# Seven of the eight late output-projection tiles as three fp32r products, in a fused attention and mixture-of-experts kernel on one Trainium2 core; the first expert tile's parts made beside them

## The chip, the core and the metric

The kernel runs on one core of a Trainium2 chip. A core has five engines that run side by side and meet by semaphores: TensorE (PE) multiplies matrices into PSUM banks, VectorE (DVE), ScalarE (ACT) and GpSimd (POOL) work on rows of 128 partitions, and SyncE (SP) issues transfers. SP, ACT and POOL each issue transfers on a queue of their own. The metric is the device time of one launch in microseconds (us).

## The reference

The layer computes, for x of shape (2, 1024, 512):

```python
xn = _layernorm(x, axis=-1)
x = x + _L0_attn_ref(xn, w_attn, b_attn, w_proj, b_proj) + _L0_ffn_ref(xn, gate_w, w1, w2)
```

The attention has 16 heads of 32 with rotary factors, a causal mask and a softmax that is scaled by 512 ** -0.5 after it; its heads are joined and projected: `o @ w_proj + b_proj`. The feed-forward part sends each of the 2048 tokens to the best 2 of 8 experts; an expert computes `silu(x w1_gate) * (x w1_up)` with 352 hidden columns and then `@ w2`, and the two results are added with the router's weights. Inputs and output are fp32.

## The kernel before, in words

The program has three blocks, one behind the other, with a barrier of all engines between them: `project_qkv` (layernorm, q, k, v, routing choice), `attend` (scores, softmax, values, and the output projection of the first sequence's eight tiles of 128 tokens), and `experts`. The change is in `experts`.

`experts` begins with the output projection of the second sequence: `LATE` = 8 tiles of 128 tokens. For each, PE multiplies `o_t` (attention output, transposed, four groups of 128 rows) by `w_proj` in four fp32 products of 512 columns (L990; the trace shows two records for each), DVE adds the residual to the bank and writes the sum back into `o_t` (L912), and ACT issues the transfer of the sum to the accumulator in HBM (L865). The banks are the four `gu` banks of the expert tiles, in turn.

Behind it come 39 expert tiles of 128 routed rows. An fp32 product is done there as three fp32r products: each operand is split into a high part (ACT casts it to fp32r, `copy`) and a low part (DVE subtracts the high part from the value), and high x high, high x low and low x high are added in PSUM. For expert tile i, PE turns the rows (`turn_rows`, L927), ACT makes `rows_hi` (L818), DVE `rows_lo` (L883); the expert's w1 is split in four pieces `w1_hi` (ACT, L822) and `w1_lo` (DVE, L890). `up(i, r, 0)` and `up(i, r, 1)` are the gate and up products, 12 of 352 columns each (L935 to L937). Then silu (ACT, L846), the product with the up half (DVE, L906), its transposition (L945, L876, L877), the down product (L953), scaling (L834) and a scatter that adds into HBM (POOL, L801). Two sets of each buffer alternate, r = i % 2.

The order on each engine is the order in which the code is written; nothing plans it. The tail of the projection is interleaved by hand with the parts of expert tile 0: at projection tile 7 ACT makes `w1_hi` and `rows_hi` of tile 0 (L860, L861), DVE makes `w1_lo` behind the add of tile 6 (L915) and `rows_lo` behind that of tile 7 (L916). PE announces a tile's expert (`announce_tile`, L976) once SP has seen its weights land; ACT waits for `tile_ready` before it reads the slot number (L738, a load of a register from memory). SP issues the weights of experts 1 and 2 after the third and the sixth residual add (L767).

Of the kernel before, what the change touches and what calls it, by code (L numbers as in the profile page):

```python
# [18 lines left out]
ALU = mybir.AluOpType  # L19
# [653 lines left out]
def experts(nc, keep, scratch, x, b_proj, w1_t, w2_t, out):  # L673
# [6 lines left out]
    with ctx:  # L680
# [12 lines left out]
        w1_lo = [m.sbuf(f"w1_lo{r}", [P, DK, 2 * I], F32R) for r in range(2)]  # L693
        gated = m.sbuf("gated", [P, I], F32)
# [20 lines left out]
        tile_ready = m.sem("tile_ready")  # L715
        gu_full, silu_done, hidden_done = m.sem("gu_full"), m.sem("silu_done"), m.sem("hidden_done")
# [92 lines left out]
        def _(act):  # L809
# [4 lines left out]
            def rows_to_sbuf(i, r):  # L814
                act.wait_ge(turned, i + 1)
                if not early(i):
                    act.wait_ge(gu_full, 2 * (i - 1))
                nc.scalar.copy(rows_hi[r][:], turn_ps[:]).then_inc(rows_hi_done, 1)  # L818
# [5 lines left out]
            def await_up_weights(i):  # L824
                if past(i, 2):
                    act.wait_ge(gu_full, (i - 1) * 2)
                act.wait_ge(tile_ready, i + 1)
# [29 lines left out]
            nc.scalar.activation(warm[:], ident[:, 0:1], ACT.Silu).then_inc(warmed, 1)  # L857
            for a in range(LATE):
                if a == LATE - 1:
                    up_weights_high(0, await_up_weights(0), range(DK))  # L860
# [10 lines left out]
        def _(dve):  # L871
# [7 lines left out]
            def rows_low(i, r):  # L879
                dve.wait_ge(rows_hi_done, i + 1)  # L880
                if not early(i):
# [3 lines left out]
            def up_weights_low(i, r, slot, ks):  # L885
                if past(i, 2):
                    dve.wait_ge(gu_full, (i - 1) * 2)
                for k in ks:
# [18 lines left out]

            for a in range(LATE):
                at = EARLY + a
                dve.wait_ge(proj_full, a + 1)  # L910

                nc.vector.tensor_tensor(o_t[:, :, at * P:(at + 1) * P], gu[a % 2][a // 2 % 2][:].rearrange("p (g t) -> p g t", t=P),  # L912
                                        res[:, at, :].rearrange("p (g t) -> p g t", t=P), ALU.add).then_inc(res_done, 1)
                if a == LATE - 2:
                    up_weights_low(0, 0, slot_at(dve, 0), range(DK))  # L915
            rows_low(0, 0)  # L916
# [4 lines left out]
        def _(pe):  # L921
# [36 lines left out]
            def tile(i, r, half):  # L958
# [7 lines left out]
                else:  # L966
                    pe.wait_ge(res_done, LATE)
# [12 lines left out]
            pe.wait_ge(ident_done, 1)  # L980
            for a in range(LATE):
# [3 lines left out]
                if a == LATE - 2:  # L985
                    announce_tile(0)
                if a == LATE - 1:
                    turn_rows(0, 0, 0)
                for g in range(NG):
                    last = nc.tensor.matmul(gu[a % 2][a // 2 % 2][:], o_t[:, g, at * P:(at + 1) * P], wp[:, g, :],  # L990
                                            start=(g == 0), stop=(g == NG - 1))
# [614 lines left out]
```

## Time and profile before

| | |
|---|---|
| runs, us | 902.1, 902.72, 905.22 (median 902.72) |
| profiled execution | 906.29 us, span 904.6 us |
| PE busy | 820.4 us, 91% of the span |
| DVE, ACT, POOL busy | 57%, 44%, 28% |
| mean granted clock of TensorE | 0.954 of full speed |

Full speed of TensorE's clock is 2.4 GHz, the lower level 1.2 GHz. Times in the rows are from the start of the span; the block `experts` opens near 562.8 and PE's first expert product is at 595.73. A timeline row gives the start, the length (of a merged group: from its first start to its last end), engine, line, operation, output and inputs, count, and in square brackets the idle time ahead of it with what ended it. PEclk is the granted clock of a stretch.

### The profile page before, as it was taken

To read this page: it belongs to the slowest core of one execution; us is meant where nothing else is said; L and a number is where in the kernel's file an instruction comes from. 1 tells how busy PE (TensorE), PEld (TensorE's weight loads), DVE (VectorE), ACT (ScalarE), POOL (GpSimd) and SP (SyncE) were. 2 spreads that over 40 slices of the span, in tenths; PEclk is the share of its full clock that TensorE was granted. 3 is DMA by queue.
4 is the path that set the end of the run, shared out by engine and by line. 5 is a ranking of instruction groups with operands and counts; after the bars stand their busy time and mean duration, and the time that the engine had idled before them with its cause. 6 is when DMAs were issued, how large, how long until landed. Compare 5 with 4: busy or idle time off the path is not lost. (4 is left out here: it accounts for less than half of the span.)

```text
span 904.6 us, 13761 instructions
## 1 busy us (share of the span) xinstructions
PE 820.4 (91%) x3973; PEld 559.8 (62%) x3974; DVE 515.3 (57%) x1334; ACT 394.8 (44%) x779; POOL 249.4 (28%) x314
## 2 busy tenths in 40 slices
PE   3889999569989999999999998979999999999990
PEld 3768989435445555555555443458778777787860
DVE  5992543395466667666666401166666666666640
ACT  3231231104445556555555630046666655556630
POOL 3782000134132424323233251002223223222220
PEclk9899999856899999999999999999999999999995
DMA  9386695894445755597671014843663664633327
GB/s 323 144 254 198 201 320 182 269 236 144 145 148 144 229 140 160 134 234 188 180 180 56 15 57 113 278 151 70 165 160 75 168 173 73 172 71 70 70 35 208
DMA packets 80477, 143.21 MB, mean 158 GB/s; under 512 B 16688, under 2 KB 30512, under 8 KB 80368
## 3 DMA queue, kind: packets, MB, share of 16 engines
q10 hardware_dynamic: 29056, 58.28, 23.8%
q1 hardware_dynamic: 43200, 65.72, 23.6%
q0 software_dynamic: 8176, 18.65, 9.8%
q8 instruction: 22, 0.36, 0.2%
q14 instruction: 23, 0.19, 0.1%
HBM read 81.21 MB, written 61.15 MB: 157 GB/s over the span
## 5 line engine op out<-in xcount | busy, mean ns | idle before, releaser
L1340 ACT ACTIVATE probs<-scores_t 128x512 f32<-128x512 f32 (+3 forms) x384 | 163.8, 492 | 148.7 <-PE scores_t L1467 136.9
L890 DVE TENSOR_TENSOR w_lo<-w,w_hi 128x704 fp32r<-128x704 f32 x156 | 131.7, 885 | 91.1 <-ACT w_hi L822 83.7
L1444 PE MATMUL maxima<-k_stack,q_stack 96*128 96x512 f32 (+3 forms) x384 | 142.2, 391 | 15.0 <-DMA q_stack<-qk_hi 9.0
L1487 PE MATMUL o_acc<-probs,v_ones 128*64 128x512 f32 (+3 forms) x768 | 149.9, 513 | 0.0
L1467 PE MATMUL scores_t<-q_stack,k_stack 98*128 98x512 f32 (+3 forms) x384 | 138.5, 386 | 7.2 <-DMA q_stack<-row_lo 5.1
L1374 DVE TENSOR_REDUCE mx<-maxima 128x1 f32<-128x512 f32 x128 | 88.2, 689 | 89.5 <-PE maxima L1444 89.3
L1370 DVE CUSTOM_DVE_ANT_0 masked_scores<-maxima,mask_m 128x128 f32<-128x128 f32 (+3 forms) x256 | 121.5, 485 | 23.8 <-PE maxima L1444 20.7
L822 ACT CAST w_hi<-w 128x704 fp32r x156 | 114.1, 783 | 34.2 <-issue 33.5
L935 PE MATMUL gu<-w_hi,rows_hi 128*128 128x352 f32 x312 | 119.7, 384 | 5.3 <-DVE rows_lo L883 4.0
L1467 PEld LDWEIGHTS scores_t<-q_stack,k_stack 98*128 98x128 f32 x384 | 73.6, 194 | 70.0 <-issue 42.7
L953 PE MATMUL down<-w,hidden_t 128*128 (+1 forms) x234 | 108.0, 597 | 0.8 <-DVE hidden_t L877 0.8
L936 PE MATMUL gu<-w_lo,rows_hi 128*128 128x352 f32 x312 | 101.5, 325 | 0.0
L937 PE MATMUL gu<-w_hi,rows_lo 128*128 128x352 f32 x312 | 101.3, 325 | 0.0
L1444 PEld LDWEIGHTS maxima<-k_stack,q_stack 96*128 96x128 f32 x384 | 77.5, 204 | 35.8 <-issue 9.5
L1285 POOL TENSOR_SCALAR_AFFINE_SELECT probs<-probs 128x256 f32<-128x256 f32 x120 | 48.4, 406 | 145.1 <-ACT probs L1340 143.5
L1487 PEld LDWEIGHTS o_acc<-probs,v_ones 128*64 128x64 f32 x768 | 47.8, 139 | 64.5 <-issue 39.6
L834 ACT ACTIVATE y<-down,tags 128x512 f32<-128x512 f32 x39 | 26.9, 689 | 107.7 <-PE down L953 58.7
L800 POOL COPY row_index<-tags 128x1 f32 (+1 forms) x39 | 8.7, 223 | 234.2 <-ACT y L834 173.3
L935 PEld LDWEIGHTS gu<-w_hi,rows_hi 128*128 128x128 f32 x312 | 59.1, 189 | 15.4 <-DVE w_lo L890 7.7
L801 POOL DMA_INDIRECT acc<-y,row_index x39 | 63.3, 1624 | 16.8 <-issue 15.4
L953 PEld LDWEIGHTS down<-w,hidden_t 128*128 128x128 f32 (+1 forms) x234 | 42.1, 190 | 39.8 <-issue 38.3
L280 ACT ACTIVATE st_hi<-bank,small 128x512 fp32r<-128x512 f32 x32 | 21.9, 687 | 101.8 <-PE bank L537 101.8
(158 smaller groups left out, 1168.9 us busy)
## 6 DMA issues: line engine op xcount, KB each, us to landing
w<-in_w_t SPq DMA_DIRECT2D x8, 1408.0 KB, 6.6
routed<-blank_row ACTq DMA_DIRECT2D x20, 514.0 KB, 6.5
rows<-routed ACTq DMA_DIRECT2D x39, 256.0 KB, 3.5
qk_hi<-st_hi SPq DMA_DIRECT2D x32, 256.0 KB, 4.7
qk_lo<-st_lo SPq DMA_DIRECT2D x32, 256.0 KB, 6.0
q_stack<-qk_hi ACTq DMA_DIRECT2D x32, 256.0 KB, 4.1
k_stack<-qk_hi ACTq DMA_DIRECT2D x26, 256.0 KB, 4.7
v_all<-o_t SPq DMA_DIRECT2D x4, 1536.0 KB, 5.7
```

What stands on the lines that cost most here:

```text
L822: nc.scalar.copy(w1_hi[r][:, k, :], w1_rows(slot, k)).then_inc(w1_hi_done, 1)
L890: nc.vector.tensor_tensor(w1_lo[r][:, k, :], w1_rows(slot, k), as_f32(w1_hi[r][:, k, :]), ALU.subtract).then_inc(w1_done, 1)
L935: nc.tensor.matmul(out, hi, w1_hi[r][:, k, cols], start=(k == 0), stop=False)
L936: nc.tensor.matmul(out, hi, w1_lo[r][:, k, cols], start=False, stop=False)
L937: last = nc.tensor.matmul(out, lo, w1_hi[r][:, k, cols], start=False, stop=(k == DK - 1))
L953: last = nc.tensor.matmul(down[r][:], hidden_t[r][0:n, k, :], w2[0:n, bass.ds(e, 1), k, :].rearrange("p o n -> p (o n)"), start=(k == 0), ...
L1340: nc.scalar.activation(probs[:, k % PR, h, 0:w], scores_t[e % RING][:, 0:w], ACT.Exp).then_inc(exp_done, 1)
L1370: nc.vector.tensor_tensor_reduce(out=masked_scores[bank][:, 0:w], in0=scores, in1=mask_m[:, CH - w:CH], scale=1.0, scalar=NEG, op0=ALU.add ...
L1374: nc.vector.tensor_reduce(to, scores, AX.X, ALU.max).then_inc(m_free, 1)
L1444: nc.tensor.matmul(mb[at % RING][:, 0:w], q_st[i][0:3 * HD, h, t * P:(t + 1) * P], k_st[i][0:3 * HD, h, c * CH:c * CH + w], start=True, st ...
L1467: last = nc.tensor.matmul(out[:, 0:w], k_st[i][0:STACK, h, j * P:(j + 1) * P], q_st[i][0:STACK, h, t0:t0 + w], start=True, stop=not diag)
L1487: last = nc.tensor.matmul(o_acc[c][2 * HD * h:2 * HD * (h + 1), CH - w:CH], v_st[i][:, j, h:h + 2, :].rearrange("p o d -> p (o d)"), probs ...
```

## The change

The first late tile keeps its four fp32 products. Tiles 1 to 7 are computed in twelve fp32r products each, like the expert tiles. Their parts are made in `experts` itself: the high part of the tile's `o_t` goes to `rows_hi`, the low part to `rows_lo` (`projected_high`, `projected_low`, one tile ahead of PE in the code), and the projection weights' parts (`wp_hi`, `wp_lo`) are laid over set 1 of `w1_hi` and `w1_lo`. So expert tile 0 may write its rows' parts only after projection tile 6 and expert tile 1 its parts only after tile 7.

Parts of expert tile 0 move ahead: `w1_hi` on ACT behind the high part of tile 6, `w1_lo` on DVE in two halves behind the adds of tiles 5 and 6, `rows_lo` ahead of the add of tile 7. The announcement of tile 0 moves from projection tile 6 to tile 4, and PE waits for the identity only at tile 7. Expert tile 0's products wait for seven adds instead of eight.

```diff
+        wp_hi, wp_lo = (t[1][:].rearrange("p k n -> p (k n)")[:, 0:NG * D].rearrange("p (g n) -> p g n", n=D) for t in (w1_hi, w1_lo))
...
+        wp_hi_done, wp_done = m.sem("wp_hi_done"), m.sem("wp_done")
+        o_hi_done, o_done = m.sem("o_hi_done"), m.sem("o_parts_done")
...
             def rows_to_sbuf(i, r):
                 act.wait_ge(turned, i + 1)
-                if not early(i):
+                if early(i):
+                    act.wait_ge(proj_full, LATE - 1 + i)
+                else:
                     act.wait_ge(gu_full, 2 * (i - 1))
...
             def await_up_weights(i):
                 if past(i, 2):
                     act.wait_ge(gu_full, (i - 1) * 2)
+                elif i == 1:
+                    act.wait_ge(proj_full, LATE)
                 act.wait_ge(tile_ready, i + 1)
...
+            def projected_high(a):
+                at = EARLY + a
+                if a > 2:
+                    act.wait_ge(proj_full, a - 1)
+                nc.scalar.copy(rows_hi[a % 2][:].rearrange("p (g t) -> p g t", t=P), o_t[:, :, at * P:(at + 1) * P]).then_inc(o_hi_done, 1)
+
+            projected_high(1)
+            for g in range(NG):
+                nc.scalar.copy(wp_hi[:, g, :], wp[:, g, :]).then_inc(wp_hi_done, 1)
             for a in range(LATE):
+                if 1 <= a < LATE - 1:
+                    projected_high(a + 1)
+                if a == LATE - 3:
+                    up_weights_high(0, await_up_weights(0), range(DK))
                 if a == LATE - 1:
-                    up_weights_high(0, await_up_weights(0), range(DK))
                     rows_to_sbuf(0, 0)
                     load_rows(2, 0)
...
             def rows_low(i, r):
                 dve.wait_ge(rows_hi_done, i + 1)
-                if not early(i):
+                if early(i):
+                    dve.wait_ge(proj_full, LATE - 1 + i)
+                else:
...
             def up_weights_low(i, r, slot, ks):
                 if past(i, 2):
                     dve.wait_ge(gu_full, (i - 1) * 2)
+                elif i == 1:
+                    dve.wait_ge(proj_full, LATE)
...
+            def projected_low(a):
+                at = EARLY + a
+                dve.wait_ge(o_hi_done, a)
+                if a > 2:
+                    dve.wait_ge(proj_full, a - 1)
+                nc.vector.tensor_tensor(rows_lo[a % 2][:].rearrange("p (g t) -> p g t", t=P), o_t[:, :, at * P:(at + 1) * P],
+                                        as_f32(rows_hi[a % 2][:]).rearrange("p (g t) -> p g t", t=P), ALU.subtract).then_inc(o_done, 1)
+
+            projected_low(1)
+            for g in range(NG):
+                dve.wait_ge(wp_hi_done, g + 1)
+                nc.vector.tensor_tensor(wp_lo[:, g, :], wp[:, g, :], as_f32(wp_hi[:, g, :]), ALU.subtract).then_inc(wp_done, 1)
             for a in range(LATE):
                 at = EARLY + a
+                if 1 <= a < LATE - 1:
+                    projected_low(a + 1)
                 dve.wait_ge(proj_full, a + 1)
...
+                if a == LATE - 4:
+                    first = slot_at(dve, 0)
+                if a == LATE - 3:
+                    up_weights_low(0, 0, first, range(0, DK // 2))
                 if a == LATE - 2:
-                    up_weights_low(0, 0, slot_at(dve, 0), range(DK))
-            rows_low(0, 0)
+                    up_weights_low(0, 0, first, range(DK // 2, DK))
+                    rows_low(0, 0)
...
                 if past(i, 2):
                     pe.wait_ge(hidden_done, i - 1)
                 else:
-                    pe.wait_ge(res_done, LATE)
+                    pe.wait_ge(res_done, LATE - 1 + i)
...
-            pe.wait_ge(ident_done, 1)
             for a in range(LATE):
                 at = EARLY + a
                 if a >= 4:
                     pe.wait_ge(res_done, a - 3)
-                if a == LATE - 2:
+                if a == LATE - 4:
                     announce_tile(0)
                 if a == LATE - 1:
+                    pe.wait_ge(ident_done, 1)
                     turn_rows(0, 0, 0)
+                bank = gu[a % 2][a // 2 % 2]
+                if a:
+                    pe.wait_ge(o_done, a)
                 for g in range(NG):
-                    last = nc.tensor.matmul(gu[a % 2][a // 2 % 2][:], o_t[:, g, at * P:(at + 1) * P], wp[:, g, :],
-                                            start=(g == 0), stop=(g == NG - 1))
+                    if a == 0:
+                        last = nc.tensor.matmul(bank[:], o_t[:, g, at * P:(at + 1) * P], wp[:, g, :],
+                                                start=(g == 0), stop=(g == NG - 1))
+                        continue
+                    if a == 1:
+                        pe.wait_ge(wp_done, g + 1)
+                    hi, lo = (t[a % 2][:, g * P:(g + 1) * P] for t in (rows_hi, rows_lo))
+                    nc.tensor.matmul(bank[:], hi, wp_hi[:, g, :], start=(g == 0), stop=False)
+                    nc.tensor.matmul(bank[:], hi, wp_lo[:, g, :], start=False, stop=False)
+                    last = nc.tensor.matmul(bank[:], lo, wp_hi[:, g, :], start=False, stop=(g == NG - 1))
                 last.then_inc(proj_full, 1)
```

PE at the opening of the block, before: fp32 products (`gu<-w_proj,o_t`), the first of them behind the identity.

```order
L920 UNCONDITIONAL_BRANCH [waits barrier_Pool_Activation_PE_DVE_SP_release]
L990 MATMUL gu<-w_proj,o_t 128x512 [waits ident3_done]
L990 MATMUL gu<-w_proj,o_t 128x512 x15
L990 MATMUL gu<-w_proj,o_t 128x512 [waits res_done]
L990 MATMUL gu<-w_proj,o_t 128x512 x3
L990 MATMUL gu<-w_proj,o_t 128x512 [waits res_done]
L990 MATMUL gu<-w_proj,o_t 128x512 x3
```

PE there after the change; `o_parts_done` counts tiles whose parts of `o_t` are made, `wp_done` the pieces of the projection weights.

```order
L961 UNCONDITIONAL_BRANCH [waits barrier_Pool_Activation_PE_DVE_SP_release]
L1035 MATMUL gu<-w_proj,o_t 128x512 x4
L1041 MATMUL gu<-w_hi,rows_hi 128x512 [waits wp_done,o_parts_done]
L1042 MATMUL gu<-w_lo,rows_hi 128x512
L1043 MATMUL gu<-w_hi,rows_lo 128x512
L1041 MATMUL gu<-w_hi,rows_hi 128x512 [waits wp_done]
L1042 MATMUL gu<-w_lo,rows_hi 128x512
L1043 MATMUL gu<-w_hi,rows_lo 128x512
L1041 MATMUL gu<-w_hi,rows_hi 128x512 [waits wp_done]
```

The wait for the identity is gone from the first product, and the second tile's products wait for parts from ACT and DVE instead.

ACT, from the table load to the first expert tile's parts, before:

```order
L857 ACT_TABLE_LOAD
L857 ACTIVATE warm<-ident 128x1 [waits ident3_done]
L865 DMA acc<-o_t 512x1x128 [waits res_done] x7
L738 TENSOR_LOAD tile_slot [waits tile_ready]
L738 ISA x2
L822 ISA
L822 COPY w_hi<-w 128x704
L822 ISA
L822 COPY w_hi<-w 128x704
```

ACT there after the change, the opening:

```order
L864 ACT_TABLE_LOAD
L864 ACTIVATE warm<-ident 128x1 [waits ident3_done]
L869 CAST rows_hi<-o_t 128x512
L873 CAST w_hi<-w_proj 128x512 x4
L884 DMA acc<-o_t 512x1x128 [waits res_done]
L869 CAST rows_hi<-o_t 128x512
L884 DMA acc<-o_t 512x1x128 [waits res_done]
L869 CAST rows_hi<-o_t 128x512 [waits proj_full]
```

and from the high part of projection tile 6 to the parts of expert tile 1, after the change:

```order
L827 ISA
L827 COPY w_hi<-w 128x704
L827 ISA
L827 COPY w_hi<-w 128x704
L884 DMA acc<-o_t 512x1x128 [waits res_done]
L869 CAST rows_hi<-o_t 128x512 [waits proj_full]
L884 DMA acc<-o_t 512x1x128 [waits res_done]
L823 CAST rows_hi<-turn_ps 128x512 [waits proj_full,rows_turned]
L815 DMA rows<-routed 128x512
L884 DMA acc<-o_t 512x1x128 [waits res_done]
L741 TENSOR_LOAD tile_slot [waits tile_ready,proj_full]
L741 ISA x2
```

Each transfer of a sum now has a cast of the next tile's `o_t` behind it on ACT, and the four `w_hi<-w` casts stand ahead of the last three transfers instead of the last one.

DVE at the end of the projection, before:

```order
L738 TENSOR_LOAD tile_slot
L738 ISA x2
L890 ISA [waits w1_hi_done]
L890 TENSOR_TENSOR w_lo<-w,w_hi 128x704
L890 ISA [waits w1_hi_done]
L890 TENSOR_TENSOR w_lo<-w,w_hi 128x704
L890 ISA [waits w1_hi_done]
L890 TENSOR_TENSOR w_lo<-w,w_hi 128x704
L890 ISA [waits w1_hi_done]
L890 TENSOR_TENSOR w_lo<-w,w_hi 128x704
L912 TENSOR_TENSOR o_t<-gu,x_rows 128x4x128 [waits proj_full]
L883 TENSOR_TENSOR rows_lo<-turn_ps,rows_hi 128x512 [waits rows_hi_done]
```

DVE there after the change:

```order
L913 ISA [waits w1_hi_done]
L913 TENSOR_TENSOR w_lo<-w,w_hi 128x704
L913 ISA [waits w1_hi_done]
L913 TENSOR_TENSOR w_lo<-w,w_hi 128x704
L936 TENSOR_TENSOR rows_lo<-o_t,rows_hi 128x512 [waits proj_full,o_hi_done]
L949 TENSOR_TENSOR o_t<-gu,x_rows 128x4x128 [waits proj_full]
L913 ISA [waits w1_hi_done]
L913 TENSOR_TENSOR w_lo<-w,w_hi 128x704
L913 ISA [waits w1_hi_done]
L913 TENSOR_TENSOR w_lo<-w,w_hi 128x704
L904 TENSOR_TENSOR rows_lo<-turn_ps,rows_hi 128x512 [waits proj_full,rows_hi_done]
L949 TENSOR_TENSOR o_t<-gu,x_rows 128x4x128 [waits proj_full]
```

The `w_lo<-w` subtractions are split by a low part and an add, and the `rows_lo<-turn_ps` subtraction stands ahead of the last add instead of behind it.

## Rows read from the trace of the kernel before

**Rows 1.** Windows: busy us of each engine, clock, DMA share, GB/s.

```profile
700.00:800.00 100.00, 100.00 (x511) 78.81 (x509) 67.49 (x112) 59.49 (x98) 26.30 (x27) 1.00 0.57 138
```

**Rows 2.** Timeline, PE: start, us, operation, count, [idle before].

```profile
563.52 24.30 PE L990 MATMUL gu<-w_proj,o_t 128*128 128x512 f32 x56 [2.63 <-POOL ident L787]
587.65 0.60 PE L927 MATMUL turn_ps<-ident,rows 128*128 128x128 f32 x4
588.09 3.60 PE L990 MATMUL gu<-w_proj,o_t 128*128 128x512 f32 x8
595.73 0.43 PE L935 MATMUL gu<-w_hi,rows_hi 128*128 128x352 f32 x1 [4.04 <-DVE rows_lo L883]
...
598.98 0.94 PE L927 MATMUL turn_ps<-ident,rows 128*128 128x128 f32 x4
...
603.21 0.40 PE L935 MATMUL gu<-w_hi,rows_hi 128*128 128x352 f32 x1 [1.30 <-DVE w_lo L890]
...
605.21 0.49 PE L945 MATMUL hid_ps<-ident,hidden 128*128 128x128 f32 x3
```

**Rows 3.** Timeline, DVE, around the last output product.

```profile
567.26 0.69 DVE L912 TENSOR_TENSOR o_t<-gu,x_rows 128x512 f32<-128x512 f32 x1 [5.64 <-PE gu L990]
...
591.17 3.30 DVE L890 TENSOR_TENSOR w_lo<-w,w_hi 128x704 fp32r<-128x704 f32 x4 [2.63 <-ACT w_hi L822]
594.39 0.68 DVE L912 TENSOR_TENSOR o_t<-gu,x_rows 128x512 f32<-128x512 f32 x1
594.99 0.68 DVE L883 TENSOR_TENSOR rows_lo<-turn_ps,rows_hi 128x512 fp32r<-128x512 f32 x1
```

**Rows 4.** Timeline, ACT and its queue, same stretch.

```profile
565.17 0.20 ACT L857 ACTIVATE warm<-ident 128x1 f32<-128x1 f32 x1
...
595.11 0.53 ACTq L865 DMA_DIRECT2D acc<-o_t  x1
596.62 1.46 ACT L822 CAST w_hi<-w 128x704 fp32r x2 [3.08 <-issue]
599.22 0.46 ACT L846 ACTIVATE gated<-gu 128x352 f32<-128x352 f32 x1 [1.14 <-PE gu L937]
```

**Rows 5.** Timeline, PE, stage one: fp32r products of 512 columns.

```profile
119.79 0.40 PE L536 MATMUL bank<-xt_lo,w_hi 128*128 128x512 f32 x1
...
125.80 0.39 PE L535 MATMUL bank<-xt_hi,w_hi 128*128 128x512 f32 x1
```

**Rows 6.** Timeline, stage one: ACT's and DVE's part making.

```profile
43.42 1.65 ACT L257 CAST w_hi<-w_raw 128x512 fp32r<-128x512 f32 x3
...
45.44 1.88 DVE L357 TENSOR_TENSOR w_lo<-w_raw,w_hi 128x512 fp32r<-128x512 f32 x3
```

**Rows 7.** Groups by form, DVE, 0 to 100 us.

```profile
L351 DVE TENSOR_TENSOR w_raw<-w_proj,o_t 128x512 f32<-128x512 f32 x8 | 7.5, 974 | 0.0
```

**Rows 8.** Timeline, POOL and SP: the block's opening, weight load.

```profile
562.81 0.21 POOL L785 MEMSET ident<- 128x128 f32 x1 [15.78 <-POOLq L1051]
...
574.84 0.37 SPq L756 DMA_DIRECT2D w<-in_w_t  x1
...
575.80 0.47 SPq L758 DMA_DIRECT2D w<-in_w_t  x1
```

**Rows 9.** Timeline, PE: other idle stretches over 1.3 us.

```profile
58.27 0.50 PE L535 MATMUL bank<-xt_hi,w_hi 128*128 128x512 f32 x1 [1.72 <-DVE st_lo L464]
...
62.66 0.51 PE L535 MATMUL bank<-xt_hi,w_hi 128*128 128x512 f32 x1 [1.34 <-DVE st_lo L464]
...
232.72 0.50 PE L1467 MATMUL scores_t<-q_stack,k_stack 98*128 98x512 f32 x1 [1.98 <-DMA q_stack<-row_lo]
...
261.52 0.61 PE L1444 MATMUL maxima<-k_stack,q_stack 96*128 96x512 f32 x1 [2.36 <-DVE mx L1370]
```

**Rows 10.** Windows: columns as in rows 1.

```profile
230.00:240.00 10.00, 8.02 (x34) 4.68 (x32) 4.37 (x14) 3.58 (x9) 2.58 (x5) 0.72 0.26 97
596.00:598.00 2.00, 2.00 (x9) 2.00 (x9) 0.45 (x1) 1.38 (x2) 0.00 (x0) 0.56 0.45 135
```

## The prediction

> **What bounds the kernel now.** I read in this order: the busy table by stretches, the timeline of TensorE (PE) around the block change, then DVE and ACT in that stretch, then older stages for prices. In the expert tiles PE is busy the whole 100 us [rows 1], one tile every 7.2 us; whatever moves the start of expert tile 1 moves the end by as much, and nothing behind it has slack to give back. So the question is when tile 1 starts. In the trace it is 603.21. Before it PE shows: idle 2.63 until the POOL identity is ready (563.52), 56 + 8 passes of the fp32 output product (64 records for 8 tiles, so 8 records a tile and 24.30 / 56 x 8 = 3.43 us a tile with the turn of 0.44 left out), end of the stream near 591.5 (588.09 + 3.43), idle 4.04 behind DVE's rows_lo, tile 0, idle 1.30 behind DVE's w_lo [rows 2]. The idle 4.04 is on DVE: four w_lo subtractions (591.17, 3.30) stand ahead of the last residual add (594.39) and rows_lo (594.99) [rows 3]. Tile 1's parts then start only after the last transfer issue of ACT at 595.11 [rows 4].
>
> **Product by product.** A 128x512 fp32r product is in stage one: 26 of them from 119.79 to 125.80 are 0.231 us apart [rows 5]. Twelve make 2.77 us against 3.43, so seven tiles save 7 x 0.66 = 4.6 us of PE work. The first tile stays fp32, and starts without the identity: the block opens at about 562.85 (POOL's first record there is 562.81 [rows 8]), not 563.52, 0.65 earlier.
>
> TensorE: Matmul & The Clock Gate, "Back-to-back issue gap", in the Trainium skill gives about 131 ns for each sustained 512-column product. By that twelve would take 1.6 us and the other two engines would pace everything; rows 5 show 231 ns here, and I do not use it.
>
> **New work on ACT and DVE.** Each product tile now needs a high part (ACT cast 128x512 from SBUF, single 0.62; three in 1.65, so 0.515 apart when queued) and a low part (DVE subtraction of SBUF tiles, three in 1.88, 0.63 apart, about 0.68 alone) [rows 6]. No trace shows the strided reads of o_t by the cast; bounds: 0.57 (a PSUM cast would be no worse) is close to 0.62, and for DVE the slow case is 0.97 for an all-SBUF 128x512 operation while other engines were busy [rows 7]. I take 0.62 and 0.68, since here POOL is idle, and keep 0.97 for a rival.
>
> The opening: ACT issues two row loads, loads its table and warms up to 565.37 [rows 4]. High part of tile 1 ready at 565.9, of the four weight pieces at 566.4, 566.9, 567.5, 568.0. DVE: low of tile 1 at 566.6, weight pieces at 567.25, 567.9, 568.5, 569.1. PE ends tile 0 at 562.85 + 3.43 = 566.28 and starts tile 1 at 567.3: stall 1.0. It then finds every piece in time and ends at 570.1. But DVE's four weight subtractions delay the residual add of tile 0 to 569.05; ACT issues its transfer (0.53) only after that add, and the high part of tile 2 stands behind the issue. 569.74 + 0.03 + 0.53 + 0.03 + 0.62 + 0.02 + 0.68 + 0.06 = 571.7. PE stalls 1.6 more.
>
> Steady: from the end of product tile a to the parts of tile a+2 there is PE to DVE 0.31 (567.26 less the end of the stream 566.95), add 0.69, issue 0.03 + 0.53, cast 0.03 + 0.62, subtraction 0.02 + 0.68, to PE 0.06: 2.97. PE works on tile a+1 meanwhile for 2.77. So it stalls 0.2 at tiles 4 and 6, 0.4 in all. The loop on DVE and ACT itself is 2.6 a tile, just below PE's 2.77.
>
> Product tile 7: ACT has four w_hi casts of 128x704 (3.0 us with the slot load ahead) between the high parts of tiles 6 and 7. They end at 585.9, high 586.4, low 587.1; PE has ended tile 6 at 585.96 and turned rows until 586.4: stall 0.8. Sum: 562.85 + 3.43 + 7 x 2.77 + 0.44 + stalls 1.0 + 1.6 + 0.4 + 0.8 = 589.9. So the product stream ends only 1.6 us earlier than 591.5: of 5.3 us saved (4.6 + 0.65), 3.8 go into new stalls.
>
> **Expert tile 0.** DVE's w_lo of this tile are split (two after the add of tile 5, two after that of tile 6, ending 589.3), rows_lo ends at 589.95. PE starts tile 0 at 590.0: the idle 4.04 is gone, 5.7 us earlier than 595.73. Its announcement is asked for at product tile 4 (577.4); SP raises it after the weight load that follows the third add. That was issued at 574.84 and took 1.4 us [rows 8]; with the third add ending at 575.5 it is raised at 577.0, in time by 0.4.
>
> **Expert tile 1: what is late next.** Its w1 parts share storage with the projection weights' parts, so ACT waits for the last product. The add of tile 7 now comes when its product ends: 589.9 + 0.31 + 0.69 = 590.95, transfer issue to 591.5, and w_hi 0.98 later (595.64 to 596.62 in the trace, with a slot load between) [rows 4]: 592.5. Two casts to 593.95, silu 0.46 [rows 4], rows_hi (0.58), two casts to 596.3, then the w_lo pair ends 597.4 and PE starts at 597.5. Tile 0 itself takes 2.0 + 0.4 + 2.0 at full clock and ends at 594.4. PE idles 3.1 us where it idled 1.30. Gain at tile 1: 603.2 - 597.5 = 5.7 us.
>
> **The clock.** The granted clock in the trace falls to its lower level (1.2 of 2.4 GHz) behind idle 1.98, 2.36 and 4.04 us, and stays up behind 1.34, 1.72 and also 2.63 [rows 2, 9, 10]. Idle 4.04 made the first half of tile 0 take 3.25 us (595.73 to 598.98) against 2.00 for tile 1's (603.21 to 605.21), and the turn 0.94 against 0.60: 1.6 in all. That loss is hidden in the old start of tile 1 only partly, because DVE and ACT set it; I count none of it twice. The new idle 3.1 ahead of tile 1 is longer than five of these six, three of the four from 1.98 up were followed by a fall, and from tile 1 on PE is the only limit: I expect one fall there. Price: between 0 and 3.4 us (in the stretch 230 to 240 the mean clock is 0.72, a longer fall), I take 1.3, a little under 1.6, as a part can pass while PE still waits. So the gain is 5.7 - 1.3 = 4.4 us.
>
> The profiled execution took 906.29 (span 904.6); the same less 4.4 is 901.9. The median of the runs is 902.72, 3.6 under it; I take the same 4.4 off that: **898.3**. A difference under 0.3% (2.7 us) cannot be told from none.
>
> **Rivals.** First, the clock stays up, as behind idle 2.63: gain 5.7, time 897.0. For it, one of the four idles from 1.98 up; against it, the other three.
>
> Second, the two helper engines become the pace. If the subtraction takes 0.97 as in rows 7, the loop is 0.69 + 0.56 + 0.65 + 0.99 = 2.9 a tile, over 2.77, the opening ends some 1.2 later and tile 7 about 2.5 later in all; with an issue of 0.61 rather than 0.53 a further 0.5. The gain is 5.7 - 3.0 = 2.7, 1.4 after the fall of the clock: 900.0 to 901.3. For it: the margin is only 0.15 a tile. Against: those slow rows stand beside POOL and heavy transfers.
>
> Third, slower: the clock falls already in the opening. Two stalls of 1.0 and 1.6 lie within 5 us. If they count as one long idle, product tiles run at half clock, 5.5 us instead of 2.77. A fall as long as that of the stretch 230 to 240 costs up to 3.4, and another of that size at tile 1 gives 6.8 against 5.7: 903.8. It decides from the point at which more than 11.4 us of PE's work run at the lower clock (each costs half of itself). Against it: the stalls 1.72 and 1.34 at 58.27 and 62.66 lie 4 us apart like these and the clock stayed up [rows 9]. The Trainium skill speaks for it in TensorE: Matmul & The Clock Gate, "A second HAM failure mode: psum-queue depth-cycling": frequent small idles between groups of products make the clock swing. Rows 9 show two that did not.
>
> Fourth, the change doesn't do what it says: the three products are not faster than the fp32 one, as when each waits for its weight load (above 0.286 each). PE would then pace the projection at 3.43, most new stalls would vanish in it, the product stream ends near 591.9 and tile 0's parts are still ready early: gain about 3.7 without, 2.4 with a fall. Against it: rows 5, the same operation at 0.231.
>
> **How the numbers follow.** Forecast 0.42, clock stays up 0.28, helpers pace 0.18, slower 0.06, not faster products 0.06. The helpers' case lies half within 0.3%. Range 895.8 to 901.4: below 897.0 by a margin for cheaper stalls (0.4 + 0.8), above to the helpers' case with a fall. Faster by over 0.3% (under 900.0): 0.42 x 0.97 + 0.28 + 0.18 x 0.4 + 0.03 = 0.79; within 0.3%: 0.16; slower 0.05.
>
> **What would show it.** Product tiles of 2.77 us on PE; stalls of about 1.0 and 1.6 ahead of product tiles 1 and 2, released by DVE, and 0.8 ahead of tile 7; almost none ahead of expert tile 0; about 3 ahead of expert tile 1, released by DVE w_lo, and half clock behind it. Tile 1 should start 5.7 us earlier (597.5), and the rest of the span should be the old 301.4 us plus what the clock takes. I am wrong if the starts of product tiles lie more than 2.9 apart after the opening, if PE waits long ahead of expert tile 0, or if something after tile 1 stalls PE that does not now.

## The result, and the profile after

In the comparison that the prediction was made for, the changed kernel has a median of 901.13 us (16 runs, 894.68 to 906.31) against 906.95 for the kernel before (16 runs, 901.9 to 912.2) on the same chips: a ratio of 0.9933, 95% interval 0.9912 to 0.9954. By the ratio that is 6 us less. Two more comparisons of the same kernel, below, gave 0.9986 (0.9953 to 1.0018) and 0.9922 (0.9897 to 0.9948). The mean of the three is 0.9947, 4.8 us of 907. The profiled execution has a span of 899.4 us, against 904.6.

All times below that are to be compared between executions are counted from POOL's first record in the block (562.81 before [rows 8], 561.21 after), since the block opened anywhere between 557.60 and 566.53 us in ten profiles of kernels that are alike up to there. I call D1 the time from there to the first product of expert tile 1: 603.21 - 562.81 = 40.40 before [rows 2, 8], 595.97 - 561.21 = 34.76 after. The timeline of PE after (start, length, operation, count, idle ahead):

```profile
561.25 5.37 PE L1035 MATMUL gu<-w_proj,o_t 128*128 128x512 f32 x8 [1.97 <-PEq L1103]
566.05 0.79 PE L1041 MATMUL gu<-w_hi,rows_hi 128*128 128x512 f32 x1
...
570.11 0.50 PE L1041 MATMUL gu<-w_hi,rows_hi 128*128 128x512 f32 x1 [0.72 <-DVE rows_lo L936]
...
575.89 0.50 PE L1041 MATMUL gu<-w_hi,rows_hi 128*128 128x512 f32 x1
...
581.73 0.47 PE L1041 MATMUL gu<-w_hi,rows_hi 128*128 128x512 f32 x1
...
584.57 0.60 PE L968 MATMUL turn_ps<-ident,rows 128*128 128x128 f32 x4
585.54 0.50 PE L1041 MATMUL gu<-w_hi,rows_hi 128*128 128x512 f32 x1 [0.37 <-DVE rows_lo L936]
...
588.40 0.37 PE L976 MATMUL gu<-w_hi,rows_hi 128*128 128x352 f32 x1
...
595.97 0.40 PE L976 MATMUL gu<-w_hi,rows_hi 128*128 128x352 f32 x1 [3.08 <-DVE w_lo L913]
...
598.99 0.84 PE L986 MATMUL hid_ps<-ident,hidden 128*128 128x128 f32 x3
```

Product tiles start at 561.25, 566.05 and 570.11, then at 573.00, 575.89, 578.75 and 581.73, which is 2.86 to 2.98 us apart; the turn of the rows is at 584.57 and tile 7 at 585.54. Expert tile 0 follows at 588.40 without an idle, where 4.04 stood before [rows 2]. The idle ahead of expert tile 1 is 3.08 instead of 1.30. The timeline of DVE after, against [rows 3]:

```profile
564.32 0.69 DVE L936 TENSOR_TENSOR rows_lo<-o_t,rows_hi 128x512 fp32r<-128x512 f32 x1 [4.31 <-ACT rows_hi L869]
564.93 2.49 DVE L942 TENSOR_TENSOR w_lo<-w_proj,w_hi 128x512 fp32r<-128x512 f32 x4
567.34 0.68 DVE L949 TENSOR_TENSOR o_t<-gu,x_rows 128x512 f32<-128x512 f32 x1
569.36 0.69 DVE L936 TENSOR_TENSOR rows_lo<-o_t,rows_hi 128x512 fp32r<-128x512 f32 x1 [1.34 <-ACT rows_hi L869]
...
584.79 0.69 DVE L936 TENSOR_TENSOR rows_lo<-o_t,rows_hi 128x512 fp32r<-128x512 f32 x1 [0.75 <-ACT rows_hi L869]
...
587.61 0.68 DVE L904 TENSOR_TENSOR rows_lo<-turn_ps,rows_hi 128x512 fp32r<-128x512 f32 x1
588.60 0.69 DVE L949 TENSOR_TENSOR o_t<-gu,x_rows 128x512 f32<-128x512 f32 x1 [0.31 <-PE gu L1043]
591.93 1.69 DVE L913 TENSOR_TENSOR w_lo<-w,w_hi 128x704 fp32r<-128x704 f32 x2 [2.64 <-ACT w_hi L827]
593.54 0.68 DVE L904 TENSOR_TENSOR rows_lo<-turn_ps,rows_hi 128x512 fp32r<-128x512 f32 x1
594.14 1.68 DVE L913 TENSOR_TENSOR w_lo<-w,w_hi 128x704 fp32r<-128x704 f32 x2
```

The four subtractions of weight pieces (564.93) hold the first residual add until 567.34. Product tile 2 waits for the subtraction at 569.36, tile 7 for that at 584.79. `rows_lo` of expert tile 0 (587.61) is ahead of the last add (588.60) now. From 591.93 DVE works without an idle until the last `w_lo` of expert tile 1 ends at 595.82, just ahead of PE's start at 595.97. ACT after, against [rows 4]:

```profile
568.05 0.61 ACTq L884 DMA_DIRECT2D acc<-o_t  x1
568.71 0.62 ACT L869 CAST rows_hi<-o_t 128x512 fp32r<-128x512 f32 x1 [2.34 <-DVE o_t L949]
...
589.32 0.53 ACTq L884 DMA_DIRECT2D acc<-o_t  x1
590.58 0.78 ACT L827 CAST w_hi<-w 128x704 fp32r x1 [3.25 <-issue]
...
591.27 0.78 ACT L827 CAST w_hi<-w 128x704 fp32r x1
...
592.77 2.82 ACT L827 CAST w_hi<-w 128x704 fp32r x4
```

The cast at 568.71 stands behind the issue at 568.05, which waited for the first add; that is the chain add, issue, cast, subtraction of the prediction. The issue at 589.32 and the first w_hi cast of expert tile 1 at 590.58 are 1.26 apart; the four casts from 592.77 are 0.68 apart and 0.78 long, and the first two of them are the last for that tile, so ACT is done with it at 594.23. The windows after (busy us of PE, PEld, DVE, ACT, POOL, then granted clock, DMA share, GB/s):

```profile
592.90:596.00 3.10, 0.03 (x1) 0.06 (x1) 3.10 (x5) 2.69 (x4) 0.00 (x0) 1.00 0.35 121
596.50:600.00 3.50, 3.50 (x16) 3.42 (x15) 1.49 (x3) 0.46 (x1) 0.00 (x0) 0.53 0.00 0
600.00:603.00 3.00, 3.00 (x18) 2.60 (x17) 2.19 (x5) 1.95 (x3) 0.00 (x0) 0.98 0.29 87
```

While PE waits for tile 1 the clock is up (1.00); it falls to its lower level (1.2 GHz) only after tile 1 has begun (0.53 on average in 596.50 to 600.00), and is up again from 600 on (0.98). Against full speed these stretches lack 3.5 x 0.47 + 3.0 x 0.02 = 1.7 us of clock. From tile 1's first product to the last down product there are 873.68 - 595.97 = 277.7 us, against 276.0 before (879.20 - 603.21).

### The profile page after: what moved, and what is told of

The parts are those of the page before. It is cut to its first block and busy times, and to the rows that moved or that the text cites. A ratio compares the mean times of both kernels' runs of the same rounds, so it can differ in the third digit from the quotient of the medians.

```text
span 899.4 us, 13854 instructions
## 1 busy us (share of the span) xinstructions
PE 817.4 (91%) x4001; PEld 565.6 (63%) x4002; DVE 521.5 (58%) x1345; ACT 401.2 (45%) x790; POOL 251.0 (28%) x314
```

## The experiments

| kernel | D1 | tile 1 to last down product | ratio to before (95%) |
|---|---|---|---|
| before | 40.40 | 276.0 | |
| changed | 34.76 | 277.7 | 0.9933 (0.9912 to 0.9954) |
| e1, fp32r products alone | 39.39 | 276.0 | 0.9962 (0.9936 to 0.9989) |
| e2, moved parts alone | 35.41 | 276.3 | 0.9949 (0.9921 to 0.9976) |
| e3, changed, transfers on SP | 31.93 | 276.1 | 0.9884 (0.9857 to 0.9911) |
| e4, changed, filler products | 34.68 | 276.1 | 0.9941 (0.9916 to 0.9965) |
| e5, e2, transfers on SP | 33.90 | 276.3 | 0.9938 (0.9900 to 0.9976) |
| e6, e3 with room of its own | 29.75 | 276.2 | 0.9869 (0.9826 to 0.9912) |
| changed, again | 34.70 | 277.6 | 0.9986 (0.9953 to 1.0018) |
| changed, third | 34.71 | 277.4 | 0.9922 (0.9897 to 0.9948) |

**e1: the products alone.** On ACT and DVE the parts of expert tile 0 go back to where they were:

```diff
-                if a == LATE - 3:
+                if a == LATE - 1:
                     up_weights_high(0, await_up_weights(0), range(DK))
-                if a == LATE - 1:
                     rows_to_sbuf(0, 0)
...
-                if a == LATE - 4:
-                    first = slot_at(dve, 0)
-                if a == LATE - 3:
-                    up_weights_low(0, 0, first, range(0, DK // 2))
                 if a == LATE - 2:
-                    up_weights_low(0, 0, first, range(DK // 2, DK))
-                    rows_low(0, 0)
+                    up_weights_low(0, 0, slot_at(dve, 0), range(DK))
+            rows_low(0, 0)
```

> The changed kernel with one part undone: the parts of expert tile 0 are made where they were before (w1_hi on ACT at projection tile 7, w1_lo on DVE behind the add of tile 6, rows_lo behind the last add); the products stay fp32r. Measure: D1, the time from POOL's first record in the block to the first product of expert tile 1; 40.4 us in the kernel before, 34.8 in the changed one. Theory (the moved parts bring most, since the saved PE time goes into new stalls): the projection ends about 1 us earlier than before, the idle of about 4 us ahead of expert tile 0 is back, D1 near 38.5 to 39.5, so 1 to 2 us of 5.6; device time 0.1 to 0.2% under the kernel before, not to be told from it. Rival (the faster products bring most of it): D1 near 36, and an idle ahead of tile 0 of under 2 us.

The timeline of PE:

```profile
562.15 0.47 PE L1036 MATMUL gu<-w_hi,rows_hi 128*128 128x512 f32 x1 [0.84 <-DVE w_lo L941]
...
566.49 0.50 PE L1036 MATMUL gu<-w_hi,rows_hi 128*128 128x512 f32 x1 [1.33 <-DVE rows_lo L935]
...
588.94 0.66 PE L971 MATMUL gu<-w_hi,rows_hi 128*128 128x352 f32 x1 [4.70 <-DVE rows_lo L903]
...
596.99 0.40 PE L971 MATMUL gu<-w_hi,rows_hi 128*128 128x352 f32 x1 [1.44 <-DVE w_lo L912]
```

The new stalls of 0.84 and 1.33 are there and the idle ahead of expert tile 0 is 4.70. D1 is 39.39, 1.0 less than before, of which 0.67 is the earlier start (0.71 behind POOL's record before, 0.04 now). The ratio looks like 3.4 us (its interval goes from 1.0 to 5.8) where 1 to 2 were expected, more than the 1.0 at D1. Its profile has 341.8 us from the opening to the end of the span, like the kernel before (341.8): behind the last down product there are 26.5 us where there were 25.4, in a stretch that the change does not touch.

**e2: the moved parts alone.** The kernel before, with the parts of expert tile 0, its announcement and the wait for the identity where the change puts them; the products stay fp32.

```diff
             for a in range(LATE):
+                if a == LATE - 3:
+                    up_weights_high(0, await_up_weights(0), range(DK))
                 if a == LATE - 1:
-                    up_weights_high(0, await_up_weights(0), range(DK))
                     rows_to_sbuf(0, 0)
...
+                if a == LATE - 4:
+                    first = slot_at(dve, 0)
+                if a == LATE - 3:
+                    up_weights_low(0, 0, first, range(0, DK // 2))
                 if a == LATE - 2:
-                    up_weights_low(0, 0, slot_at(dve, 0), range(DK))
-            rows_low(0, 0)
+                    up_weights_low(0, 0, first, range(DK // 2, DK))
+                    rows_low(0, 0)
...
-                    pe.wait_ge(res_done, LATE)
+                    pe.wait_ge(res_done, LATE - 1 + i)
...
-            pe.wait_ge(ident_done, 1)
...
-                if a == LATE - 2:
+                if a == LATE - 4:
                     announce_tile(0)
                 if a == LATE - 1:
+                    pe.wait_ge(ident_done, 1)
```

> The kernel before with the other part alone: all eight projection tiles stay fp32, and the parts of expert tile 0, its announcement and the wait for the identity are moved as in the changed kernel. Theory: the eight products stay back to back, 8 x 3.43 + 0.44 from 0.05 behind the opening, the idle ahead of expert tile 0 is under 0.5 us, and tile 1 starts 7.5 us behind the last projection product: D1 35.3 to 36, so some 4.5 to 5 of the 5.6 us; ratio to the kernel before 0.993 to 0.997. Rival (the products bring it): D1 above 38.

```profile
559.37 24.27 PE L995 MATMUL gu<-w_proj,o_t 128*128 128x512 f32 x56 [1.96 <-PEq L1056]
...
594.74 0.40 PE L940 MATMUL gu<-w_hi,rows_hi 128*128 128x352 f32 x1 [2.87 <-DVE w_lo L891]
```

The fp32 products run back to back from 559.37, no idle stands ahead of expert tile 0, and D1 is 35.41: 5.0 of the 5.65 us, of which 0.67 is the earlier start again (0.71 behind POOL's record before, 0.04 here). The rival, that the products bring the gain, has fallen.

**e3: the issue out of ACT's way.** The eight transfers of the sums move to SP.

```diff
-                act.wait_ge(res_done, a + 1)
-                act.dma_start(acc_rows[at], o_t[:, :, at * P:(at + 1) * P]).then_inc(acc_started, 16)
...
+            load_weights(0)
+            for a in range(LATE):
+                at = EARLY + a
+                sp.wait_ge(res_done, a + 1)
+                sp.dma_start(acc_rows[at], o_t[:, :, at * P:(at + 1) * P]).then_inc(acc_started, 16)
+                if a == 2:
+                    load_weights(1)
+                    announce(0)
+                if a == 5:
+                    load_weights(2)
```

> The changed kernel with the eight transfers of the sums issued by SP instead of ACT, so that ACT's cast of the next tile's high part waits for neither the residual add nor the issue (0.53 us). Theory (the new stalls come from the chain add, issue, cast, subtraction, and the start of expert tile 1 from the last add and issue ahead of its casts): stalls ahead of projection tiles 2, 4 and 6 vanish (1.2, 0.3 and 0.3 us in the changed kernel), the one ahead of tile 7 shrinks below 0.5, expert tile 1 starts 6 to 6.5 us behind the last projection product instead of 7.6: D1 31 to 32.5, against 34.8. Time 0.2 to 0.4% under the changed kernel. Rival (DVE paces the projection, and tile 1 waits for DVE in any case): D1 above 34.

```profile
566.57 5.37 PE L1037 MATMUL gu<-w_proj,o_t 128*128 128x512 f32 x8 [1.97 <-PEq L1105]
...
574.52 0.39 PE L1043 MATMUL gu<-w_hi,rows_hi 128*128 128x512 f32 x1
...
580.67 0.47 PE L1043 MATMUL gu<-w_hi,rows_hi 128*128 128x512 f32 x1 [0.55 <-SPq L766]
...
592.24 0.38 PE L978 MATMUL gu<-w_hi,rows_hi 128*128 128x352 f32 x1
...
598.46 0.40 PE L978 MATMUL gu<-w_hi,rows_hi 128*128 128x352 f32 x1 [1.64 <-DVE w_lo L915]
```

The stalls ahead of product tiles 2 and 7 are gone, and expert tile 1 starts 6.2 us behind the end of the projection (592.24 to 598.46) instead of 7.6 (588.40 to 595.97). D1 is 31.93, 2.8 less than in the changed kernel. The ratio is 0.5% under that of the changed kernel where 0.2 to 0.4 was expected; the two ratios come from different comparisons. One thing I had not expected: PE idles 0.55 at product tile 4 for SP. SP announces expert 0 only behind the weights of expert 1, as before, but now has the issue of a transfer ahead of those. The prediction had put the margin of this announcement at 0.4 us in the changed kernel; it held there. The clock fell in the opening of this execution too, and here it shows: product tile 2, which waits for nobody, starts 7.99 us behind the opening, against 7.46 in e6 below, where the clock stayed up. SP's issue of the third sum, for which that announcement waits, ends 0.39 later than in e6 (12.14 and 11.75 us behind the opening). So I estimate that some 0.4 us of e3's D1 is the clock.

**e4: fill the idle.** Twelve products whose result is overwritten stand between the halves of expert tile 0.

```diff
+                if isinstance(i, int) and i == 0:
+                    for k in range(3 * DK):
+                        nc.tensor.matmul(gu[1][0][:, 0:I], rows_hi[0][:, k % DK * P:(k % DK + 1) * P],
+                                         w1_hi[0][:, k % DK, 0:I], start=(k == 0), stop=(k == 3 * DK - 1))
                 up(i, r, 1)
```

> The changed kernel with twelve filler products of 352 columns put between the two halves of expert tile 0 (their result is overwritten; nothing reads it), to fill 2.0 of the 3.1 us for which PE waits ahead of expert tile 1. Theory (the idle makes the clock fall in tile 1): D1 stays within 0.4 us of 34.8, the clock stays up behind it, and the stretch from tile 1's first product to the end of the span is 301 to 302 us instead of 303.4; time about 0.2% under the changed kernel. Rival (the fall comes from something else, or costs nothing at the end): the stretch stays at 303.4.

```profile
590.39 2.17 PE L1017 MATMUL gu<-w_hi,rows_hi 128*128 128x352 f32 x12
...
595.65 0.40 PE L976 MATMUL gu<-w_hi,rows_hi 128*128 128x352 f32 x1 [1.18 <-DVE w_lo L913]
```

and the window behind:

```profile
595.00:600.00 5.00, 4.35 (x29) 4.35 (x30) 3.95 (x7) 3.31 (x6) 0.00 (x0) 1.00 0.06 4
```

D1 stays (34.68), the idle is 1.18, the clock stays up, and the stretch from tile 1 to the last down product is 276.1 us instead of 277.7. So the fall behind the idle of 3.1 us costs 1.6 us. By the measure of the expectation, from tile 1 to the end of the span, it is 302.15 against 303.43, or 1.3 us; I count to the last down product because what lies behind it differs by up to 0.8 us between executions of the changed kernel alone (25.7, 26.5 and 25.9). The ratio, 0.9941, does not resolve this: its interval spans 4.4 us.

**e5: fp32 products, transfers on SP.** e2 with the edit of e3.

> The kernel with fp32 projection products and the moved parts (e2), and the transfers of the sums issued by SP as in e3. It tells what the fp32r products are worth once ACT no longer stands in their way. Measure: D1, the time from POOL's first record of the block to the first product of expert tile 1 (before 40.4, changed kernel 34.8, e2 35.4, e3 31.9). Theory (in the changed kernel the saved PE time was eaten by the chain over ACT's issue; freed of it the three products pay their arithmetic): projection ends at 28.0 as in e2, tile 1 starts 6.2 to 6.3 us behind it as in e3, D1 34.2, so e3 is 2.3 us better by its products. Rival (the products pay nothing in any case, SP's issue is the whole gain of e3): D1 near 32.

```profile
559.10 24.34 PE L997 MATMUL gu<-w_proj,o_t 128*128 128x512 f32 x56 [1.97 <-PEq L1058]
...
583.71 3.60 PE L997 MATMUL gu<-w_proj,o_t 128*128 128x512 f32 x8
...
592.96 0.40 PE L942 MATMUL gu<-w_hi,rows_hi 128*128 128x352 f32 x1 [1.29 <-DVE w_lo L893]
```

D1 is 33.90. Against e3's 31.93 the fp32r products are worth 2.0 us where ACT's issue is out of the way, and 35.41 - 34.76 = 0.65 where it is not. The 2.0 are rather too few: e3 also carries the estimated 0.4 us of the clock and the wait for SP.

**e6: room of its own for the weight parts.** e3 with three edits; DVE's half of the tile gets the same two changes (no wait for the last projection product, and `first`).

```diff
-        wp_hi, wp_lo = (t[1][:].rearrange("p k n -> p (k n)")[:, 0:NG * D].rearrange("p (g n) -> p g n", n=D) for t in (w1_hi, w1_lo))
+        wp_hi, wp_lo = (m.sbuf(name, [P, NG, D], F32R) for name in ("wp_hi", "wp_lo"))
...
-                    load_weights(1)
                     announce(0)
+                    load_weights(1)
...
-                elif i == 1:
-                    act.wait_ge(proj_full, LATE)
...
-                    up_weights_high(1 - r, slot, range(0, DK // 2))
+                    first = DK if isinstance(i, int) and i == 0 else DK // 2
+                    up_weights_high(1 - r, slot, range(0, first))
```

> e3 with three edits on what then waits last: the projection weights' parts get buffers of their own (16 KB a partition) in place of set 1 of w1_hi and w1_lo, so that expert tile 1's w1 parts wait for no projection product and all four are made ahead of the silu and the rows' parts of tile 0 and 1; and SP announces expert 0 ahead of issuing the weights of expert 1 (in e3 PE idles 0.55 us for that announcement at projection tile 4). Theory (what is left ahead of tile 1 is the w1 parts' wait for the last projection product, and then 0.5 us of DVE work): no idle at projection tile 4, idle ahead of expert tile 1 0.3 to 0.8 us instead of 1.64, D1 29.7 to 30.5 against 31.9 of e3. Time 0.1 to 0.3% under e3, 1.2 to 1.5% under the kernel before. Rival (the silu of tile 0 and the rows' parts set the start of tile 1, not the w1 parts): D1 above 31.

```profile
564.21 0.47 PE L1041 MATMUL gu<-wp_hi,rows_hi 128*128 128x512 f32 x1 [0.84 <-DVE wp_lo L942]
...
567.12 0.50 PE L1041 MATMUL gu<-wp_hi,rows_hi 128*128 128x512 f32 x1
...
584.14 0.38 PE L976 MATMUL gu<-w_hi,rows_hi 128*128 128x352 f32 x1
...
589.41 0.43 PE L976 MATMUL gu<-w_hi,rows_hi 128*128 128x352 f32 x1 [0.76 <-DVE rows_lo L905]
```

DVE at the same place:

```profile
584.34 0.69 DVE L949 TENSOR_TENSOR o_t<-gu,x_rows 128x512 f32<-128x512 f32 x1 [0.30 <-PE gu L1043]
585.45 3.30 DVE L912 TENSOR_TENSOR w_lo<-w,w_hi 128x704 fp32r<-128x704 f32 x4 [0.42 <-ACT w_hi L832]
588.67 0.68 DVE L905 TENSOR_TENSOR rows_lo<-turn_ps,rows_hi 128x512 fp32r<-128x512 f32 x1
```

The idle at product tile 4 is gone, the four w_lo of tile 1 run in one piece from 585.45, and the idle ahead of tile 1 is 0.76, now released by rows_lo. D1 is 29.75, 10.65 us less than before. The time is 0.9869 of the kernel before (a median of 895.58 us in six runs), the lowest ratio of all versions, though its interval overlaps that of e3; from the opening to the end there are 332.2 us against e3's 333.9. The three edits were made together, so what each brings is not shown. The product stream ends 584.14 - 559.66 = 24.48 us behind the opening; with fp32 products in e5 it ends at 583.71 + 3.43 - 559.06 = 28.08. So 3.6 of the 4.6 us that the products save are there once neither ACT's issue nor SP's announcement is in the way, and the stall ahead of product tile 1, which begins 564.21 - 559.70 - 3.43 = 1.1 us late, takes the rest.

**The changed kernel twice more.**

> The changed kernel once more, on the chip and in the rounds of the other two, to tell whether the loss at the lower clock is the same in each execution. Theory: D1 34.3 to 35.0 again; whether the clock falls ahead of expert tile 1, behind an idle of 3.1 us, varies from one execution to the next, since the idle stretches of 1.97 and 2.87 us were once followed by a fall and once not: the stretch from tile 1's first product to the last down product is 276.0 without a fall and 277.7 with one. Ratio 0.991 to 0.996. Rival (the fall always follows this idle): 277.7 again, which one run cannot refute.

```profile
564.57 3.67 PE L1035 MATMUL gu<-w_proj,o_t 128*128 128x512 f32 x8 [1.97 <-PEq L1103]
569.08 0.47 PE L1041 MATMUL gu<-w_hi,rows_hi 128*128 128x512 f32 x1 [0.84 <-DVE w_lo L942]
...
573.43 0.50 PE L1041 MATMUL gu<-w_hi,rows_hi 128*128 128x512 f32 x1 [1.34 <-DVE rows_lo L936]
...
599.23 0.40 PE L976 MATMUL gu<-w_hi,rows_hi 128*128 128x352 f32 x1 [3.09 <-DVE w_lo L913]
```

> The changed kernel a third time, since its two comparisons so far (0.9933 and 0.9986) differ by more than their intervals allow for one and the same kernel. Theory (the block starts and ends as in the two profiles, D1 34.7 and 1.7 us for the clock's fall, so the true gain is 3.6 to 4.4 us of 906, and the comparisons scatter with the start of the block, which lay between 557.6 and 566.5 us in profiles of kernels that are alike up to there): D1 34.6 to 34.8, ratio 0.992 to 0.999, and the mean of the three near 0.9955. Rival (the gain of the first comparison, 6 us, is the true one and something in the block is missing from the sum): ratio 0.992 to 0.994 and open to end under 336 us.

```profile
565.30 5.37 PE L1035 MATMUL gu<-w_proj,o_t 128*128 128x512 f32 x8 [1.97 <-PEq L1103]
...
574.16 0.50 PE L1041 MATMUL gu<-w_hi,rows_hi 128*128 128x512 f32 x1 [0.75 <-DVE rows_lo L936]
...
599.97 0.63 PE L976 MATMUL gu<-w_hi,rows_hi 128*128 128x352 f32 x1 [3.11 <-DVE w_lo L913]
```

D1 is 34.70 and 34.71, and the fall behind the idle of 3.1 us was there both times (277.6 and 277.4 us behind it), so the varying fall that the first of these expectations looked for was not seen. The ratio of that run, 0.9986, is also outside the expected 0.991 to 0.996. The clock at the opening was not the same: in the second execution all tiles ran at full clock, with stalls of 0.84 and 1.34; in the first and third it fell during tile 0 and that tile's slowness took the place of the first stall (one of 0.75 is left). Tile 2 starts 8.90 us behind the opening either way. As for the rival in the expectation of the third, its ratio is in the rival's range, but the profile is not: from the opening to the end there are 338.0 us, where the rival wanted under 336. Why the second comparison and the third have intervals that do not meet is not settled. They ran on different chips (0 and 12), and whether the chip matters was not tested: e5 and e6, compared on chip 0 too, agree with their profiles within their intervals (5.6 and 11.9 us by the ratio, 5.5 and 9.6 from the opening to the end). The profiles show a spread of 8.9 us in the opening of the block, with the code ahead of it unchanged, which is larger than the gain; how much of it enters a comparison was not measured.

## Why the prediction was right

The forecast was 4.4 us less and 0.79 for faster; the first comparison gave 6 us, the three together 4.8, and the profile 341.8 - 338.2 = 3.6 us from the opening to the end (3.0 and 3.8 in the two repeats, all against one profile of the kernel before). The absolute figure, 898.3, was counted from a median of 902.72 in three runs. The kernel before has 906.95 in the 16 runs of the comparison, and 4.4 less than that is 902.5, against the measured 901.13. That the three comparisons lie on both sides of the forecast (6, 1 and 7 us) and average close to it is in part luck; what bears it out is the chain inside the block, term by term.

- **The product tile.** Forecast 2.77 us from [rows 5]; in the trace the 12 products from 581.73 to the turn at 584.57 take 2.84. They are 0.23 us apart, as in [rows 5], but for the first, which is 0.31 ahead of the second. The rival in which the products are no faster has fallen.
- **The opening and the stalls.** Predicted were 1.0, 1.6, 0.2, 0.2 and 0.8 (3.8 in all), each as the time by which a tile starts later than 3.43 (fp32) or 2.77 us behind the start of the one before it. The idle in brackets is less than that, since it is counted from the end of a product's record (0.39 long, where the products start 0.23 apart). In the terms of the prediction the repeat at full clock has 569.08 - 564.57 - 3.43 = 1.08 and 573.43 - 569.08 - 2.77 = 1.58 for the first two. Tile 7's was too large in the forecast: 585.54 - 584.57 - 0.44 = 0.53. Beyond these stalls the tiles from the second on take 0.7 us more than 2.77 each, summed up, where 0.4 was forecast. The two misses cancel: expert tile 0 starts 27.19 us behind the opening, forecast 27.2. The start of tile 2 was met as well, 8.90 against 571.7 - 562.81 = 8.9.
- **The helpers' pace.** The rival with a subtraction of 0.97 has fallen: DVE's took 0.69, the cast 0.62. The sign set for it, product tiles more than 2.9 us apart, was too tight, for the prediction's own sum has 2.97 at tiles 4 and 6. Measured are 2.86 to 2.98, and 3.81 from tile 6 to tile 7 with the turn between.
- **Expert tile 0** has no idle ahead of it, as forecast. e1 shows that without the move it has 4.7.
- **Expert tile 1.** Forecast D1 597.5 - 562.81 = 34.7 with an idle of 3.1; measured 34.76 and 3.08. That it is met to the tenth is partly luck. The forecast let ACT set the pace to the end: last cast 6.4 us behind the product stream (596.3 - 589.9), then two subtractions in 1.1. Measured are 594.23 - 588.40 = 5.8 for the cast, and from 591.93 on DVE is busy throughout with two `w_lo`, `rows_lo` and two more `w_lo` (3.9 us), so its own queue sets the end, 7.4 behind the stream where 7.5 was forecast. How the wait begins was named rightly: e3, in which the issue ahead of the casts is gone, starts tile 1 1.35 us sooner behind the stream, and e6, which also gives the parts room of their own, brings 2.2 us more at D1 together with its other edits.
- **The clock.** One fall ahead of tile 1 was forecast at 1.3 us; it cost 1.6 (e4) to 1.7 (against the stretch before). This is the term that was too small, by 0.3 to 0.4. The forecast took less than 1.6 "as a part can pass while PE still waits", and none did: the clock was up through the wait (1.00 in 592.90 to 596.00) and fell after tile 1 had begun. The rival without a fall was wrong in all three executions profiled. The slower rival needed a fall at the opening and a price for it: the fall came in two of three executions, and cost nothing, because tile 2 waits for DVE until 8.90 in any case. I had not seen that the wait at tile 2 hides it; without that price the rival could not come true. (Its price of 3.4 us is the whole of the fall from 234 to 242 us of the kernel before; the mean of 0.72 in 230 to 240 that is given for it makes 2.8.)
- **The end.** From the last down product to the end of the span there are 25.7 us after and 25.4 before; in the other profiles 25.8 to 26.5. This was no term of the sum. It takes 0.3 us of the profile's 3.6, and its scatter is a good part of the difference between 3.0 and 3.8.

What the title of the change suggests, that faster products make the kernel faster, is a small part of it: of 5.65 us at tile 1 the moved parts with the earlier start bring 5.0, the products 0.65 on top of that. e3, e5 and e6 show where most of their 4.6 us of PE work went: into waits for ACT, whose cast of the next tile stood behind the issue of the last tile's transfer, and into the stall ahead of tile 1, whose parts are made only once the block is open.

## What to carry to other kernels

When the main engine's work shrinks, draw the loop of its helpers with everything in their queues, transfer issues and the waits of these issues too; if the loop is within a few tenths of the new tile time, the gain will turn into stalls, and the cheapest remedy is to issue the transfers from an engine that nothing waits for. Then ask what else that engine announces, since it is now late by the same issues. Work for the first tile of the next phase is best put into the idle time of helpers in the phase before, and storage that the two phases share decides how far ahead that can go. For changes of a few microseconds count from a fixed event ahead of the change in each profile, rather than from the total.

## What the runs showed of the hardware

- The granted clock behind the same idle of 1.96 to 1.97 us at the opening fell in three of nine profiles (the changed kernel's first and third, e3) and stayed up in six. The same idle can be followed by either. It fell in three of three behind 3.08 to 3.11 us, behind 4.04 (before) and behind 4.70 (e1), and not behind 2.87 (e2).
- A fall costs 1.6 us where PE alone sets the end (the changed kernel against e4). It costs nothing where a helper sets the next start for long enough: product tile 2 starts 8.90 us behind the opening with and without it. With that wait gone (e3 against e6) the same tile starts 0.5 us later.
- In the changed kernel the first fp32r product of 512 columns behind a wait is 0.34 us ahead of the next one (570.11 to 570.45), where the others are 0.23 apart.
